# Attention values with their high and low parts side by side, and the sums and additions moved between engines

## What is computed

```python
x = x + tanh(g_xattn[0]) * xattn(layernorm(x), ctx)      # 16 heads of 16, softmax over 77
#   q = x Wq + bq, k = y Wk + bk, v = y Wv + bv; out = softmax(q k^T / 4) v
#   xattn = relu(out W1 + b1) W2 + b2
x = x + tanh(g_ffn[0]) * experts(layernorm(x))           # 8 experts, top 2
#   s = max(x gate_W + gate_b, 1e-4); p = softmax(s); w = max(p, 0.1), normed over the top 2
#   out = sum over the top 2 of w_e (x W_e + b_e), halved
```

## Time and profile before

| | |
|---|---|
| median of 3 runs | 976.85 us (972.44 to 977.27) |
| profiled execution | 977.29 us, span 975.6 us |
| busy in the span | PE 928.8 (95%), PEld 675.4 (69%), DVE 844.3 (87%), ACT 720.8 (74%), POOL 641.7 (66%) |
| granted TensorE clock | 0.972 on the mean |
| chain that ended last, by engine | PE 80%, DVE 12%, issue 5%, ACT 2% |
| attend's three products | 1024 matmuls each, 98.1 + 96.3 + 96.4 us busy |

### The profile page before, as it was taken

How to read it: one execution, slowest core, us unless ns; L and a number is a source line. 1 busy time by engine, 2 the same in 40 slices (tenths; PEclk the granted TensorE clock), 3 DMA queues, 4 the chain that set the end, 5 groups by cost and what they waited for, 6 DMA issues and landing times.

```text
span 975.6 us, 26129 instructions
## 1 busy us (share of the span) xinstructions
PE 928.8 (95%) x9410; PEld 675.4 (69%) x9410; DVE 844.3 (87%) x2107; ACT 720.8 (74%) x1517; POOL 641.7 (66%) x793
## 2 busy tenths in 40 slices
PE   3668999999999999999999999999999999999997
PEld 2556777777777777777777777777777777777763
DVE  5776898899888889988888898898889988988875
ACT  4745787777878777787887778788777878877661
POOL 5435566677766667776666777666678766667743
PEclk8677999999999999999999999999999999999999
DMA  7000000000000000000000000000000000000000
GB/s 201 28 12 3 15 25 26 26 23 21 20 15 27 25 26 23 22 19 15 26 25 26 23 26 15 15 26 26 27 23 26 16 15 26 25 13 13 12 12 22
DMA packets 17471, 24.61 MB, mean 25 GB/s; under 512 B 2798, under 2 KB 8896, under 8 KB 17344
## 3 DMA queue, kind: packets, MB, share of 16 engines
q1 hardware_dynamic: 17344, 22.94, 7.6%
HBM read 14.54 MB, written 8.39 MB: 24 GB/s over the span
## 4 chain that ended last, share of the span: by engine, by line
PE 80%; DVE 12%; issue 5%; ACT 2%; DMA 0%; POOLq 0%; DVEq 0%; POOL 0%; ACTq 0%
PE e L742 29%; PE g L742 16%; PE t L925 7%; PE t L791 6%; DVE h_lo L1291 4%; DVE acc L1213 4%; PE s L876 3%; PE g L942 3%; PE s L812 3%; PE s L813 3%; PE s L811 2%; PE g L751 2%; PE g L887 2%; PE g L952 1%; PE t L910 1%
## 5 line engine op out<-in xcount | busy, mean ns | idle before, releaser
L374 POOL TENSOR_TENSOR p_lo<-p_f,p_hi 77x512 f16<-77x512 f32 x160 | 184.2, 1166 | 207.9 <-ACT p_hi L560 207.9
L742 PE MATMUL e<-we_hi,x2T_lo 128*128 128x512 f16 x496 | 189.2, 381 | 0.0
L742 PE MATMUL e<-we_hi,x2T_hi 128*128 128x512 f16 x496 | 188.9, 381 | 0.0
L742 PE MATMUL e<-we_lo,x2T_hi 128*128 128x512 f16 x496 | 188.8, 381 | 0.0
L559 ACT ACTIVATE p_f<-t 77x512 f32<-77x512 f32 x256 | 152.4, 595 | 16.9 <-PE t L791 10.0
L1213 DVE SCALAR_TENSOR_TENSOR acc<-e,comb,acc 128x256 f32<-128x256 f32 x307 | 146.3, 477 | 13.9 <-PE e L742 10.6
L560 ACT ACTIVATE p_hi<-t 77x512 f16<-77x512 f32 x256 | 152.3, 595 | 0.0
L1258 DVE TENSOR_REDUCE row_max<-s 128x6 f32<-128x462 f32 (+1 forms) x192 | 107.7, 574 | 4.6 <-PE s L876 2.8
L638 ACT ACTIVATE scaled<-e,comb 128x256 f32<-128x256 f32 x126 | 56.3, 474 | 72.5 <-PE e L742 72.5
L811 PE MATMUL s<-v_hi,p_lo 77*128 77x17 f16 x1024 | 98.1, 172 | 7.7 <-DVE p_lo L1196 4.6
L811 PEld LDWEIGHTS s<-v_hi,p_lo 77*128 77x128 f16 x1024 | 84.0, 96 | 27.9 <-issue 10.5
(11 more groups left out here) (194 smaller groups left out, 2847.6 us busy)
## 6 DMA issues: line engine op xcount, KB each, us to landing
x_sb<-in_x SPq DMA_DIRECT2D x32, 256.0 KB, 2.6
out<-acc SPq DMA_DIRECT2D x32, 256.0 KB, 2.0
we_f<-in_L_ffn_expert_W SPq DMA_DIRECT2D x2, 1024.0 KB, 9.5
y_sb<-in_ctx SPq DMA_DIRECT2D x32, 57.8 KB
w_f<-in_L_xattn_W SPq DMA_DIRECT2D x2, 512.0 KB, 7.3
wq_f<-in_L_xattn_Wq SPq DMA_DIRECT2D x1, 256.0 KB, 4.2
wkv_f<-in_L_xattn_Wk SPq DMA_DIRECT2D x1, 192.0 KB, 2.9
wkv_f<-in_L_xattn_Wv SPq DMA_DIRECT2D x1, 192.0 KB, 3.8
```

The costliest lines, as they stand in the source:

```text
L374: pool.tensor_tensor(p_lo[:, r].rearrange("m h n -> m (h n)"), p_f[:, r, :], p_hi[:, r].rearrange("m h n -> m (h n)"), ALU.subtract).then_ ...
L742: mm = pe.matmul(out_ap, a, c, start=(first and i == 0), stop=(last and i == n - 1))
```

## The change

The high and low parts of the values lie side by side in one tile, v_both, per head 16 high values, the ones, 16 low values: 33 columns. attend multiplies hi by all 33 and then adds lo by all 33 to the same place. A bank of 512 columns has room for 15 such tiles and one of 17, so 15 of 16 tiles of a half take two products (lo by the low values comes in with it) and the last one three, as before. ScalarE copies the low columns of a half (low_values_copy) into SBUF, and VectorE adds them to the high ones in PSUM (add_low_values), ahead of the reciprocals and the normalisation, one each per half.

The order changes with it. On VectorE add_expert(7) goes between the two halves. On TensorE experts(1) goes ahead of output_transposes, so that combT_transposes, scores_for_max(1) and expert_biases follow these. On GpSimd add_scaled goes from the middle of the step after to the close of the row's own step, behind the second norm's scales, and x_with_bias behind these too. In the first row p_low(7) is GpSimd's. The last row's final sum is VectorE's, one tile at a time, and its store is two DMAs. At the start the second half of the experts' largest weights, W1's and the power of two are taken at the end of step 0, and the weights are split in step 1; at the end the row's gate, combT and biases change places with its experts.

```diff
+PACK = DV + DH
+PACKED = T * H // 2 - 1
...
+                if has(s, -1) and m == 0:
+                    p_low(m, FIRST_LOW)
...
-                if has(s, -3):
-                    add_scaled(f, fu)
+                if has(s, -3) and f < B - 1:
                     add_biases(f, fu)
...
-                if has(s, 1):
-                    x_with_bias(n, nu)
                 if has(s, -1):
                     second_norm_scale(m, 0)
                     second_norm_scale(m, 1)
+                if has(s, 1):
+                    x_with_bias(n, nu)
+                if has(s, -2):
+                    add_scaled(e, eu)
...
+            def low_values_copy(b, half):
+                act.wait_ge(av_done, 8 * b + 4 * half + 4)
+                at_least(act, low_values_added, 2 * (b - 1) + half + 1)
+                parts = S[half][:, 0:PACKED * PACK].rearrange("p (a d) -> p a d", d=PACK)
+                act.activation(low_values[:, half], parts[:, :, DV:PACK], ACT.Copy).then_inc(low_values_copied, 1)
...
+                if s == 1:
+                    first_layer_high()
+                    experts_high((0,))
...
                 if front:
                     highT_copies(b)
+                if mid:
+                    low_values_copy(m, 0)
+                if front:
                     q_stack_high(b)
+                if mid:
+                    low_values_copy(m, 1)
+                if front:
                     k_stack_high(b)
...
+                if s == 1:
+                    experts_high((2, 3))
+                    gate_and_biases_high()
                 if mid:
                     oT_high(m)
...
-                        pe.matmul(dst, lo, v_hi[:, u, h, :], start=True, stop=False)
-                        pe.matmul(dst, hi, v_lo[:, u, h, :], start=False, stop=False)
-                        mm = pe.matmul(dst, hi, v_hi[:, u, h, :], start=False, stop=True)
+                        if a < PACKED:
+                            dst = S[half][:, a * PACK:(a + 1) * PACK]
+                            pe.matmul(dst, hi, v_both[:, u, h, :], start=True, stop=False)
+                            mm = pe.matmul(dst, lo, v_both[:, u, h, :], start=False, stop=True)
+                        else:
...
+                if first and s <= B:
+                    experts(e, eu, 1, s - 2)
                 if mid:
                     output_transposes(m)
                 if first and s <= B:
...
                 if front:
                     scores_for_max(b, 1)
                 if first and s <= B:
-                    experts(e, eu, 1, s - 2)
                     expert_biases(e)
...
+            def add_low_values(b, half):
+
+                dve.wait_ge(low_values_copied, 2 * b + half + 1)
+                parts = S[half][:, 0:PACKED * PACK].rearrange("p (a d) -> p a d", d=PACK)
+                dve.tensor_tensor(parts[:, :, 0:DH], parts[:, :, 0:DH], low_values[:, half], ALU.add).then_inc(low_values_added, 1)
...
+                if mid and m > 0:
                     p_low(m, 7)
+                if mid:
+                    add_low_values(m, 0)
                     reciprocals(m, 0)
                     normalise(m, 0, 0)
                     normalise(m, 0, 1)
...
+                if last:
+                    add_expert(f_pair, f, fu, 7, 0, s - 3)
+                    add_expert(f_pair, f, fu, 7, 1, s - 3)
+                if last and f == B - 1:
+                    add_last_biases(f, fu, 1)
+                if mid:
+                    add_low_values(m, 1)
                     reciprocals(m, 1)
                     normalise(m, 1, 0)
                     normalise(m, 1, 1)
...
                 if s == 0:
-                    weights_low()
-                    experts_low(0)
+                    output_bias()
+                    largest_expert_weights(1)
+                    largest_weights()
+                    power_of_largest()
```

More of the change, by code:

```diff
@@ L47 @@
 EARLY = 7 + 5
-CONSTS = EARLY + 1 + 8
+CONSTS = EARLY + 1 + 7
 PARTS = 4
@@ L51 @@
 VECTOR_LOW = (0, 2, 7)
+FIRST_LOW = 7
 QUAD = 32
@@ L281, in store @@
             def store(pair, u, b):
-                sp.wait_ge(acc_done, b + 1)
-                sp.dma_start(out_pairs[pair, u], acc[:, u]).then_inc(stored[u], 16)
+                if b < B - 1:
+                    sp.wait_ge(acc_done, b + 1)
+                    sp.dma_start(out_pairs[pair, u], acc[:, u]).then_inc(stored[u], 16)
+                    return
+                for t in range(T):
+                    sp.wait_ge(acc_done, b + 1 + t)
+                    sp.dma_start(out_pairs[pair, u][:, t], acc[:, u, t]).then_inc(stored[u], 16)
             def step(pair, u, s):
@@ L318, in _ @@
             run(step)
-            for u in range(2):
-                sp.wait_ge(stored[u], 16 * (B // 2))
+            sp.wait_ge(stored[0], 16 * (B // 2))
+            sp.wait_ge(stored[1], 16 * (B // 2 + T - 1))
         @block.gpsimd
@@ L799, in attend @@
                     pe.wait_ge(max_taken, 6 * b + 6)
-                if g in VECTOR_LOW:
-                    pe.wait_ge(p_lo_vector, len(VECTOR_LOW) * b + VECTOR_LOW.index(g) + 1)
+                if b == 0 and g == FIRST_LOW:
+                    pe.wait_ge(p_lo_pool, len(POOL_LOW) + 1)
+                elif g in VECTOR_LOW:
+                    pe.wait_ge(p_lo_vector, len(VECTOR_LOW) * b + VECTOR_LOW.index(g) + (0 if b else 1))
                 else:
-                    pe.wait_ge(p_lo_pool, len(POOL_LOW) * b + POOL_LOW.index(g) + 1)
+                    pe.wait_ge(p_lo_pool, len(POOL_LOW) * b + POOL_LOW.index(g) + (2 if b else 1))
                 r, half = g % RING, g // 4
@@ L807, in attend @@
                     for t in range(T):
-                        at = (t * (H // 2) + h % (H // 2)) * DV
+                        a = t * (H // 2) + h % (H // 2)
                         hi, lo = p_hi[:, r, e, t * P:(t + 1) * P], p_lo[:, r, e, t * P:(t + 1) * P]
-                        dst = S[half][:, at:at + DV]
-                        pe.matmul(dst, lo, v_hi[:, u, h, :], start=True, stop=False)
-                        pe.matmul(dst, hi, v_lo[:, u, h, :], start=False, stop=False)
-                        mm = pe.matmul(dst, hi, v_hi[:, u, h, :], start=False, stop=True)
+                        if a < PACKED:
[3 more added lines that the diff above has]
+                        else:
+                            dst = S[half][:, a * PACK:a * PACK + DV]
+                            pe.matmul(dst, lo, v_both[:, u, h, 0:DV], start=True, stop=False)
+                            pe.matmul(dst[:, 0:DH], hi, v_both[:, u, h, DV:PACK], start=False, stop=False)
+                            mm = pe.matmul(dst, hi, v_both[:, u, h, 0:DV], start=False, stop=True)
                 mm.then_inc(av_done, 1)
@@ L992, in step @@
                     transposes_y(pair, b, u)
-                if first and s <= B:
+                if s == 2:
+                    experts_weights()
+                if first:
                     gate_scores(e, eu)
@@ L1215, in add_expert, with add_last_biases @@
                                          op0=ALU.mult, op1=ALU.add).then_inc(expert_added, 1)
+            def add_last_biases(b, u, t):
+                dve.wait_ge(scaled_added, 2 * b + 2)
+                dve.wait_ge(expert_added, 2 * len(ADDED) * (b + 1) - 2 * (T - 1 - t))
+                dve.tensor_tensor(acc[:, u, t], acc[:, u, t], bias_sum[:, u, t], ALU.add).then_inc(acc_done, 1)
             def kv_with_bias(b):
@@ L1380, in step @@
                     xnT_low(b)
+                if s == 1:
+                    weight_scales()
                 if front:
@@ L1434, in step @@
                     add_expert(f_pair, f, fu, 6, 1, s - 3)
+                if last and f == B - 1:
+                    add_last_biases(f, fu, 0)
+                if s == 1:
+                    experts_low(1)
+                if mid and m > 0:
+                    p_low(m, 7)
                 if mid:
-                    p_low(m, 7)
+                    add_low_values(m, 0)
                     reciprocals(m, 0)
@@ L1443, in step @@
                     normalise(m, 1, 1)
-                if last:
-                    add_expert(f_pair, f, fu, 7, 0, s - 3)
-                if last:
-                    add_expert(f_pair, f, fu, 7, 1, s - 3)
                 if front:
                     take_max(b, 0)
+                if s == 1:
+                    experts_low(2)
                 if mid:
                     oT_low(m)
-                if s == 0:
-                    weight_scales()
                 if front:
```

62 lines of the change are left out of this document (30 added, 32 removed).

## The result

The changed kernel takes 1028.22 us (median of 4 runs, 1026.57 to 1028.5) beside 974.64 of the kernel before on the same chip: 1.054 times as long, 95% interval 1.051 to 1.0565. The forecast was 985, the range ended at 1018; what came is rival 2, with something on top.

The account below looks back on a forecast made before the run. TensorE was taken as the bound, VectorE just behind. From 977.3 us: +13.3 for steady steps, -5 start, +1 for steps 2 and 32, -1 end gave 985.6, rounded down to 985; range 956 to 1018.

Parts of the forecast that it names:

- rival 2: VectorE's p_low(7) loses to GpSimd's k_block, ending about 1.2 us later every step: 35 us, 1020; chance 0.25.
- The choice among the cases: Chances for the whole kernel: forecast (985) 0.40, saving kept (963 to 954) 0.35, p_low(7) losing to GpSimd (1020) 0.25.
- The lock: VectorE with two SBUF inputs and GpSimd reading SBUF exclude each other a whole instruction; first holds; loss one k_block.
- GpSimd's moved steps: add_scaled and x_with_bias at the step's close fit, 3.8 us, into GpSimd's 4.57 of idleness; nothing charged.
- The products: In attend on TensorE, 30 of 96 matmuls a row go, at 25.3 ns each: 0.76 us a step saved.
- The sum of the halves: ScalarE's copy takes 0.46 us; VectorE's add 0.40, of which 0.33 until the next can start.
- The path with the new order: From p_low(7) to mlp_up: TensorE idles about 1.05 us ahead of expert_biases, mlp_up(0) starts 0.85 later.
- Back from that: Gate to p_low(7) 0.10 shorter, h_lo stall of 0.29 gone: steady step 0.46 us longer, +13.3 us over 29.
- Start and end: Start -5 us (-2 to -9), steps 2 and 32 +0.5 each, end -1.
- Rival 1: Saving kept, output_transposes starting by about 487.5: at most 0.6 us a step, 954, at half 963; chance 0.35.

Follow-up runs that it names:

- the two cures: Changed kernel with GpSimd's first k_block waiting for p_low(7): 991.3 us; changed kernel with qhT copied ahead of khT: 992.22 us.
- the kernel without collisions: Changed kernel with GpSimd's first k_block waiting for p_low(7) and x_with_bias moved behind the split of the values: 985.59 us.
- the products alone with qhT first: Changed kernel with every change of order in the steady step taken back and qhT copied ahead of khT: 965.21 us.
- the last run: Changed kernel with experts(1) and add_expert(7) ordered as before, x_with_bias behind the values' split, and qhT copied ahead of khT: 950.84 us.

## Why the prediction was wrong, step by step

- **The choice among the cases: wrong.** Rival 2 came, at 0.25 the least likely of the three. Its price was right: 29 x 1.2 = 35 us against the 37 and 36 that the two cures gave back. Two things were wrong with its chance. First, the 0.15 us taken as p_low(7)'s lead were read at k_block's recorded start, which is only where p_low(6) ends. That lead is 0.15 in the changed kernel too (504.60 and 504.75), and p_low(7) loses there. What moved is khT, from 0.15 to 0.39 ahead of p_low(6)'s end, past the 0.22 at which the turn changes; p_low(6), which the prediction had coming forward with khT, kept its place, 0.19 behind p_low(7)'s start. Second, the paragraph's own numbers already decided the case: khT 0.3 to 0.4 earlier and p_low(7) 0.10 earlier is a shift of 0.2 to 0.3 against a lead of 0.15. Measured, khT's shift against p_low(7) was 0.24 (from 0.04 after its start to 0.20 ahead). The range took in only half of rival 2 for the same reason.
- **The lock: right, but not by the recorded starts.** Where p_low(7) loses it waits for nearly a whole k_block (1.15 to 1.22 us of 1.25), as the Trainium skill, SBUF — State Buffer, section "SBUF: two separate sides", has it. The Trainium skill's rule there, that the first to start holds, does not come out of the recorded starts: by these VectorE was first each time. The prediction took step 2 for one whole k_block; its 2.35 hold 0.38 of p_low(6), k_block and the 0.25 of comb_stack behind it, up to 85.50.
- **GpSimd's moved steps: charged at nothing, wrong in kind, small in size.** The two additions did fit into GpSimd's pause ahead of p_low(1), but only GpSimd's side was looked at. x_with_bias shuts out the second xn for 0.94 us, worth 0.22 of a step, some 6 us in all. The gain on the other side was right: the h_lo pair 0.75 instead of 1.47, and TensorE's wait for h_lo is gone; the moves alone make the kernel before 0.5% faster.
- **The products: right.** From 504.99 to 505.37 there are 15 spacings, 25.3 ns each with 33 columns, as with 17.
- **The sum of the halves: right.** The add took 0.40 and 0.32 until the next (0.40 and 0.33 forecast), the copy 0.38 (0.46).
- **The path with the new order: right, a little short.** Without the collisions, counted from p_low(7)'s start: o complete 3.66 (513.20 + 0.49; forecast 3.71), output_transposes 4.02 (3.99), idle 1.09 (1.05), expert_biases 6.12 (5.99), mlp_up 6.87 (6.64). That the idleness comes with the new order is shown by the run that put experts(1) and add_expert(7) back, in which it is gone, 25 us faster.
- **Back from that: right.** From the gate's first matmul to p_low(7) it is 8.33 (526.58 to 534.91) instead of 8.44: 0.11 (0.10 forecast). The step without collisions is 28.89, 0.52 longer than before; forecast 0.46.
- **Start and end: the sum right, by two errors.** The start gave 5.1 with one p_low(7) of 2.34 in step 2; without collisions p_low(7) of step 3 comes at 105.48, 10.1 earlier than before, where -5 + 0.5 was forecast and 9 was the bound. The end became 1.7 longer (0.9 without collisions) instead of shorter. That the 985.59 of the kernel without collisions meets the forecast of 985 closer than its terms do is luck.
- **Rival 1: its condition can be met, its price only with more.** In the products alone with qhT first, output_transposes start 2.93 after p_low(7), 487.39 on the prediction's clock, and TensorE doesn't wait at expert_biases. That kernel takes 965, but the step is only 0.08 shorter than before (28.29); of its 12.2 us of span 8.1 are the start's (p_low(7) of step 3 at 107.43), 2.2 the steps' and 1.8 the end's. Where the 0.76 us go: 0.24 into the wait for o; and of the five attends that lie between the gate and p_low(7) only 0.10 shows, as that stretch is 8.33 there (8.44 before). GpSimd has four p_low in a row in it without a pause (4.80), and these, it is argued and was not tried, hold it. But rival 1 counted on GpSimd's moves as well, and the last run, which has them with x_with_bias at its early place, has steps 0.53 shorter than before (27.84), of the 0.6 that it allowed: the saving could be kept, with the order of before and qhT first.

## What to carry to other kernels

Where VectorE and GpSimd follow each other closely on SBUF, don't read a lead off the recorded starts. Look how long before the end of GpSimd's running instruction the last input of its next one is there: here the turn changed near 0.22 us. If a change shifts that input by more than the room that is left, take the turn as the forecast. A saving on TensorE can bring inputs forward on other engines, and so turn such a race; here the cheapest cure was the order of two copies on a third engine. And when an operation moves on GpSimd, look up what VectorE does at the new place, as well as whether GpSimd has room.

## What was not expected of the hardware

- Whether khT is there 0.15 or 0.39 us ahead of p_low(6)'s end decides over 1.2 us, in every steady step alike: the kernel before stood some 0.07 us from the turn, and khT copied early cost it 44 us.
- GpSimd's addition of 1.27 us shuts out a VectorE operation on float32 in SBUF with a single tensor input too (xn, 0.41 to 1.35).
